# A decoder block on one core: output projections in other banks, and the square roots of the first half's values computed by ScalarE

## The reference, cut to what matters

```python
# x: (L=4, positions 256, D=256); 16 heads of 16; l runs over the batch axis
x = silu(x_prev * conv_w[:, 0] + x * conv_w[:, 1])
q, k, v, g = silu(x @ Wq), x @ Wk, x @ Wv, x @ Wg     # q and k are then rotated
...                                                   # routing: softmax, argmax, counts
qk = (q_exp @ k_exp.T) * HDK ** -0.5 * tril
o = qk @ v
o = (o - mean(o)) / sqrt(var(o) + 1e-5)               # per head
out = (silu(g) * o) @ Wout
x = layernorm(x + out)
```

## Time and profile before

| | us |
|---|---|
| median of 3 runs | 209.92 |
| lowest and highest of them | 209.91, 210.71 |
| the profiled execution | 210.53 |
| its span in the profile | 208.7 |
| PE busy | 173.5 |
| VectorE busy | 117.5 |
| GpSimd busy | 96.5 |
| ScalarE busy | 88.0 |

### The profile page before, as it was taken

One profiled execution on the slowest core, in us unless ns is written; L12 is line 12 of the kernel. 1 busy time (PEld: TensorE's weight loads), 2 busy tenths in 40 slices (PEclk: granted clock), 3 DMA queues, 4 the chain that ended last, 5 costly groups with the idle time before them and its releaser, 6 DMA issues.

```text
span 208.7 us, 3665 instructions
## 1 busy us (share of the span) xinstructions
PE 173.5 (83%) x1196; PEld 120.5 (58%) x1196; DVE 117.5 (56%) x324; ACT 88.0 (42%) x223; POOL 96.5 (46%) x179
## 2 busy tenths in 40 slices
PE   0799995989999998988886798997686978895870
PEld 0375773446666776676775677964342644664750
DVE  0144654476997774895631204621957947988441
ACT  1126746045433534524353242674445064445432
POOL 8522027427689506272645006533636514455362
PEclk9999969699999999999999999999889999999999
DMA  6999200200000001015364871411200000001102
GB/s 209 305 314 365 105 3 0 101 2 3 3 3 0 3 0 51 4 46 170 113 228 179 279 274 50 138 67 32 68 2 5 24 0 0 0 2 50 50 5 102
DMA packets 16405, 17.50 MB, mean 84 GB/s; under 512 B 3041, under 2 KB 13825, under 8 KB 16385
## 3 DMA queue, kind: packets, MB, share of 16 engines
q1 hardware_dynamic: 11504, 12.75, 18.5%
q10 hardware_dynamic: 4112, 2.41, 3.9%
q0 software_dynamic: 768, 2.10, 3.2%
HBM read 7.82 MB, written 5.77 MB: 65 GB/s over the span
## 4 chain that ended last, share of the span: by engine, by line
PE 65%; ACT 8%; issue 8%; DVE 8%; POOL 6%; DMA 2%; POOLq 0%; ACTq 0%; SPq 0%; DVEq 0%
PE bank L1465 23%; PE bank L1552 7%; PE bank L1713 6%; PE bank L1698 5%; PE bank L1460 5%; PE bank L1804 4%; PE bank L1580 3%; PE bank L1788 3%; DMA x_sb<-in_x 2%; PE bank L1805 2%; PE bank L1574 1%; POOL xs_d L452 1%; POOL probs L507 1%; DVE probs L1061 1%; PE bank L1518 1%
## 5 line engine op out<-in xcount | busy, mean ns | idle before, releaser
L1465 PE MATMUL bank<-f_w,oT 128*128 128x512 f32 (+4 forms) x80 | 29.8, 522 | 5.7 <-ACT oT L767 3.6
L1061 DVE TENSOR_TENSOR probs<-bank,con 128x512 f32<-128x512 f32 x32 | 20.7, 684 | 12.0 <-PE bank L1552 11.9
L393 POOL TENSOR_TENSOR rsin<-qk,rope_tab 128x256 f32<-128x256 f32 x16 | 11.8, 759 | 29.3 <-ACT qk L633 29.3
L1465 PEld LDWEIGHTS bank<-f_w,oT 128*128 128x128 f32 x80 | 15.0, 197 | 17.7 <-issue 8.4
L1552 PE MATMUL bank<-qx,kT 32*128 32x256 f32 x128 | 18.8, 411 | 2.5 <-ACT ctxT L679 2.3
L1465 PE MATMUL bank<-w_qk,xT 128*128 128x512 f32 x32 | 18.6, 710 | 1.4 <-ACT qk L633 0.8
L463 POOL DMA_INDIRECT yg<-ys_d,pos x8 | 7.9, 993 | 20.2 <-DMA ys_d<-qkr 18.7
L1552 PEld LDWEIGHTS bank<-qx,kT 32*128 32x128 f32 x128 | 11.6, 192 | 9.6 <-issue 7.9
L1698 PE MATMUL bank<-xsT,slot_w 128*128 128x128 f32 x112 | 14.0, 276 | 2.5 <-issue 2.5
L1162 DVE TENSOR_TENSOR rsin<-rcos,bank 128x512 f32<-128x512 f32 (+1 forms) x8 | 5.0, 620 | 19.4 <-ACT rcos L740 19.4
L1713 PE MATMUL bank<-slot_w,rsin 128*128 128x256 f32 x56 | 13.6, 382 | 2.1 <-DVE rsin L1162 1.7
(11 more groups left out here) (162 smaller groups left out, 385.9 us busy)
## 6 DMA issues: line engine op xcount, KB each, us to landing
slot_w<-ctxT SPq DMA_DIRECT2D x14, 256.0 KB, 2.4
xs_d<-xs SPq DMA_DIRECT2D x2, 896.0 KB, 8.5
xs<-xs_d SPq DMA_DIRECT2D x6, 256.0 KB, 3.3
ys_d<-qkr ACTq DMA_DIRECT2D x6, 256.0 KB, 2.5
x_sb<-in_x SPq DMA_DIRECT2D x4, 256.0 KB, 6.4
ctx_sb<-in_ctx SPq DMA_DIRECT2D x1, 1024.0 KB, 9.9
out<-x_sb SPq DMA_DIRECT2D x8, 128.0 KB, 1.7
con<-shape_constants SPq DMA_DIRECT2D x1, 410.0 KB, 3.7
```

Source lines behind the costliest of these rows:

```text
L393: eng.tensor_tensor(dst[:, :, s, :], src[:, :, 1 - s, :], tab[:, :, s, :], ALU.mult)\
L1061: eng.tensor_tensor(probs[:, i % 2, :, :].rearrange("p (f r h) n -> p f r h n", f=KT, h=2)[:, :, g, :, :], bank[3 + g % 2][:, :].rearrange ...
L1465: last = eng.matmul(dst, lhsT[:, k, :], w[:, k, :], start=(k == 0), stop=(k == KT - 1))
```

## The change

Four edits. The output projections use banks 4, 7, 2, 4, 6 for groups 0 to 4, and wait for what used these banks last: groups 1 and 2 for the last convolution (bank 7 and 2 hold transposed tiles until then), group 3 for finish(0) and finish(1), group 4 for the values of the last tile (bank 6). ready_roots leaves its early place. A ready_roots and root_values(0, 1) stand between square_values(1) and copy_step(4), and a second ready_roots stands between copy_step(7) and finish(0). head_rstd(0, 1) takes the short form that groups 2 to 4 had, and so waits for ScalarE's root.

```diff
         def out_bank(g):
-            return [4, 4, 4, 7, 2][g]
+            return [4, 7, 2, 4, 6][g]
...
             silu_qk(3)
             copy_ctxT(2)
-            ready_roots()
             copy_ctxT(3)
...
             scale2(7)
             square_values(1)
+            ready_roots()
+            root_values(0, 1)
             copy_step(4)
             keep_prev(5)
             silu_conv(6)
...
             square_values(2)
             copy_step(7)
+            ready_roots()
             finish(0)
             finish(1)
             root_values(2, 2)
...
                 if c:
                     eng.wait_ge(S_("f_gated"), L)
-                if not c:
-                    inverse_root(frs[:, s], fvar[:, s], (l1 - l0) * H, 1.0 / HD, LN_EPS, "f_rstd")
-                    return
                 n = (l1 - l0) * H
                 v, a = newton[:, 0, 0:n], newton[:, 1, 0:n]
                 link(eng.tensor_scalar(v, fvar[:, s], 1.0 / HD, LN_EPS, ALU.mult, ALU.add))
-                eng.wait_ge(S_("f_root"), ROOTS[g0] - 1)
+                eng.wait_ge(S_("f_root"), ROOTS[g0])
                 link(eng.reciprocal(frs[:, s], froot[:, s]))
...
                 if g == 0:
                     eng.wait_ge(S_("probs"), 4 * TILES)
                 elif g < 3:
-                    eng.wait_ge(S_("out_done"), 2 * g)
+                    eng.wait_ge(S_("conv"), 2 * TILES)
+                elif g == 3:
+                    eng.wait_ge(S_("out_done"), 2)
                 else:
-                    eng.wait_ge(S_("conv"), 2 * TILES)
+                    eng.wait_ge(S_("fv_copied"), TILES)
```

## The result

The changed kernel takes 212.49 us (median of 4 runs, 211.75 to 212.60), the kernel before 209.95 beside it: 1.0105 times as long, interval 1.0072 to 1.0137. That is 2.5 us slower, where 1.1 us faster was forecast, and outside the range of 206.5 to 211.5. The profiled executions lie closer together than the medians: 211.75 with a span of 209.8 after, 210.53 with 208.7 before, so the two spans differ by 1.1 us. Where executions of one kernel differ by whole stretches at half clock, a ratio with its interval is taken over those at the higher clock and a median over all, so the two need not match.

What follows compares the result with a forecast made beforehand. The prediction took PE as the bound, with 65% of the chain. From the profiled 210.53 us, -3.9 - 0.8 + 3.9 - 0.3 = -1.1 gave 209.4, and the median 0.61 lower, 208.8; range 206.5 to 211.5.

Steps and rivals of the forecast that it cites:

- Early removal: Around scores(0, 0) and proj_qk(5): two loads, two PE waits and a half-clock stretch go; -3.9 us, bounds -2.2 and -3.9.
- Rival 1: PE's half clock at 37 us stays, so only 2.2 us are gained early; 211.3 us, chance 0.20.
- The stretch at 149 us: PE's half clock from about 149.7 to 153.1 us may vanish or stay; -0.8 us, bounds -1.7 and +1.0.
- the stretch near 160 us: Another half-clock stretch on PE may appear near 160 us, where the same pattern recurs; upper bound +1.0 us.
- The middle roots: Before copy_step(4): two ScalarE loads start project_step(5) 3.2 us later, at half clock; +3.9 us at project_step(6)'s end.
- The banks: In the tail project_out(1) and (2) stop waiting, but group 2's transposes wait for fgo; gain 0.3 us, bounds 0 and 1.0.
- rival 3: In the tail PE idles about 2.4 us for fgo; half clock slows sum_pairs(4) by 1.0 us; 210.6 us, chance 0.15.
- VectorE's roots: head_rstd(0, 1) is ready 0.3 us sooner, which buys nothing because conv_step(6) behind it waits for keep_prev(5).
- the price at 173.7: Half clock at project_step(5) after PE idles 4.6 us; costs 1.5 us, bounds 0.9 and 2.3.

## Why the prediction was wrong, point by point

**Early removal, right.** Forecast -3.9 with two loads, two waits and one stretch at half clock; the idle stretch came out at 0.89 us (0.87 forecast), proj_qk(4) at 1.98 us, proj_qk(5) without a wait. Between scores(0, 0) and proj_qk(5) the changed kernel gains 2.6 us, and its idle stretch is 1.4 us shorter: 4.0 us. The median says 4.8 us; the 0.8 us beyond the terms were not forecast (in the trace 0.5 lie ahead of the edit and 0.4 at sum_pairs(1)). That it is handed on to the end is shown by the second part, 42.9 us with and without. Rival 1, the slower case of the forecast, did not happen.

**The stretch at 149 us, not right.** I took -0.8 for half a chance that it vanishes. It did not vanish in any trace with the idle time unfilled. In the changed kernel and five others project_step(2) takes 5.02 us as before; in the other five of the changed traces it takes 3.33, and project_step(4), which took 4.19, takes 5.9 instead: the stretch near 160 us that the text allowed for, at the same 1.7 us. Only the filled idle time removed it. So the term was worth 0, and that the early removal gained 4.8 us where this term and the one above add up to 4.7 is luck.

**The middle roots, the step that failed.** "That this is one load and not two is seen from copy_step itself, where tanh, silu and copies follow each other without any." Those rows show that with silu's set loaded the tanh needs nothing. They say nothing of which set is loaded when the tanh comes first with the root's set in place. It was one that did not serve silu, and the third load made the delay of project_step(5) 4.58 us (5.96 - 1.38) instead of 3.2. The slack of 0.72 us ahead of project_step(6) was taken up as forecast. The half clock behind the idle stretch was forecast, at 1.5 us with bounds 0.9 and 2.3; it measured 9.05 - 7.04 = 2.0 us in the trace, and 2.2 us by filling the stretch. In all: 4.58 - 0.72 + 2.0 = 5.9 us for the forecast 3.9. With silu's set first PE's idle stretch was the forecast one, so the rest of the sum for this place was sound.

**The banks, the wrong branch.** I forecast -0.3 and gave the half clock in the tail (rival 3) a chance of 0.15, though the same text said that PE's idle stretch would grow to about 2.4 us and that 2.29 us had brought the fall at 37 us. By those two rows it was the likely case: idle was 2.66 to 2.78 us and sum_pairs(4) ran slowly in five of the six profiles that show this stretch unfilled. The transposes came 0.05 us sooner, and the cost was 1.3 to 1.7 us. That transposes of group 2 would wait for GpSimd's fgo was right, and is why nothing was gained.

**VectorE's roots.** Ready 0.3 us sooner and of no use, as forecast: conv_step(6) waited 3.28 us for ScalarE. The experiment with conv_step(6) first shows that 1.16 of their 2.8 us are hidden behind the wait for keep_prev(5) when they stand first.

**The sum**, with the medians: forecast -4.7 + 3.9 - 0.3 = -1.1; measured -4.8 + 5.8 + 1.7 = +2.7. Both misses have the same sign: 1.9 us at the middle roots (1.4 the third load, 0.5 the clock behind the longer idle stretch) and 2.0 us at the banks (1.7 of cost, which the filled tail ties to the clock, and 0.3 of gain that did not come). The range had a slip besides: it took 0.2 us for the upper bound of the price at 173.7, but 2.3 lies 0.8 above the 1.5 in the sum, so its slower end would have been 212.1. The measured 212.49 lies beyond that too, and no case had a third load.

## What to carry to other kernels

Count the loads of function sets by walking ScalarE's list in order and asking at each activation which set would be loaded for this function, and not whether some set holds the next one too (seen here for one case, tanh and then silu with the root's set loaded); rows taken with another set loaded don't answer that, and an activation of one column with the rarer function can choose the set. A wait taken away from PE where another one stands directly behind it only joins two idle stretches into a longer one, and on PE that can cost more than it saves. Where PE must idle for 1 to 6 us, a few matmuls on constants into a free bank, sized to end before the wait does, are cheap to try.

## What the runs showed of the hardware

- Idle stretches of PE of 2.3 to 6 us were followed by half clock (1.2 instead of 2.4 GHz) in 12 of 13 cases in these traces (three of 2.29 us, four of 3.98 to 5.96, six of 2.66 to 2.78), and filling idle time kept the clock full behind it in all four kernels that did so. The cost of such a wait on PE was its length plus 1.3 to 2.2 us. Stretches of 1.4 us had no such effect at 165 and 184 us in the early removal's trace. Around 143 to 156 us, where waits of 1.15, 0.63, 1.15 and 1.28 us follow each other, half clock came in all twelve traces with these waits unfilled, in seven at project_step(2) and in five at project_step(4).
- In one execution of six the idle stretch of 2.66 us in the tail was followed by full clock, and the stretch at 26 to 31 us, where nothing was changed, was at half clock in some executions and at full in others. Single runs of one kernel differ by several microseconds (205.75 to 212.97 for the banks alone, at a mean granted clock of 0.986 and 0.960), which is why parts of the trace were compared and not only totals. What decides it was not tried.
- A load took 1.28 us everywhere and, where ScalarE was at work, began about 0.02 us behind the activation ahead of it; no further time around it was seen, in the kernel before or in any other.
